# Attention inside a pre-norm block: weighing the shared key tile with split products

## What is computed

```
attn = jnp.where(valid, q @ k.T * scale, neg)      # valid: q_pos-128 < k_pos <= q_pos
attn = softmax(attn)
out  = attn @ v                                    # per head
x    = x + out @ wo
x    = x + ffn(layernorm(x))                       # ternary weights, exact gelu
```

## Time and profile before

| | us |
|---|---|
| median of 3 runs | 352.41 (350.9 to 352.82) |
| profiled execution, its own time | 355.15 |
| its span in the trace | 353.4 |
| TensorE busy | 340.2 (96% of the span) |
| VectorE busy | 270.7 (77%) |
| ScalarE busy | 206.6 (58%) |
| GpSimd busy | 224.0 (63%) |

### The profile page before, as it was taken

How to read it: one execution, slowest core, us unless ns; L and a number is a source line. 1 busy time by engine, 2 the same in 40 slices (tenths; PEclk the granted TensorE clock), 3 DMA queues, 4 the chain that set the end, 5 groups by cost and what they waited for, 6 DMA issues and landing times.

```text
span 353.4 us, 6926 instructions
## 1 busy us (share of the span) xinstructions
PE 340.2 (96%) x2410; PEld 315.9 (89%) x2410; DVE 270.7 (77%) x605; ACT 206.6 (58%) x628; POOL 224.0 (63%) x182
## 2 busy tenths in 40 slices
PE   7887989999999999999999999999999999989996
PEld 7876768999999999999999999999999999968986
DVE  4875867768876887889888987787788876878682
ACT  2424855687677556655665566656665566466280
POOL 2325878667767678898898897676767487230400
PEclk9989989999999999999999999999999999999999
DMA  7826465543333333333333333333322232000001
GB/s 220 213 58 173 127 166 152 130 105 78 91 86 81 81 86 87 92 89 92 89 91 89 91 90 91 92 90 76 91 54 56 57 89 61 0 3 0 32 30 59
DMA packets 29025, 31.25 MB, mean 88 GB/s; under 512 B 3392, under 2 KB 20288, under 8 KB 28992
## 3 DMA queue, kind: packets, MB, share of 16 engines
q1 hardware_dynamic: 28992, 30.82, 34.0%
HBM read 12.98 MB, written 1.05 MB: 40 GB/s over the span
## 4 chain that ended last, share of the span: by engine, by line
PE 85%; DVE 6%; POOL 3%; DMA 3%; issue 1%; ACT 1%; SPq 0%; POOLq 0%; DVEq 0%
PE PR L397 23%; PE OT L476 13%; PE SC L449 12%; PE VO L414 12%; PE VO L431 12%; PE PT L460 4%; PE PR L504 2%; PE VO L511 2%; PE SC L504 2%; DMA swapped<-by_sin 2%; POOL gT_lo L992 1%; PE SC L511 1%; POOL turn L987 1%; DMA xres<-in_x 1%; DVE stats L726 1%
## 5 line engine op out<-in xcount | busy, mean ns | idle before, releaser
L992 POOL TENSOR_TENSOR gT_lo<-turn,gT_hi 128x512 fp32r<-128x512 f32 x62 | 82.2, 1325 | 47.2 <-ACT gT_hi L622 47.0
L987 POOL TENSOR_TENSOR turn<-turn,swapped 128x512 f32<-128x512 f32 x62 | 80.2, 1293 | 25.7 <-DMA swapped<-by_sin 25.1
L627 ACT ACTIVATE probs<-SC,negmax 128x128 f32<-128x128 f32 x128 | 45.8, 363 | 80.6 <-DVE negmax L790 80.6
L801 DVE TENSOR_TENSOR probsT<-PT,mask_sb 128x512 f32<-128x512 f32 x64 | 44.1, 690 | 40.2 <-PE PT L460 40.1
L476 PE MATMUL OT<-probsT,v_sb 128*128 128x128 f32 x450 | 60.4, 276 | 1.6 <-DVE probsT L801 0.9
L476 PEld LDWEIGHTS OT<-probsT,v_sb 128*128 128x128 f32 x450 | 55.2, 191 | 2.9 <-DVE probsT L801 2.8
L634 ACT ACTIVATE probs<-probs,rinv 128x128 f32<-128x128 f32 x128 | 44.5, 394 | 19.1 <-DVE rinv L795 19.0
L397 PE MATMUL PR<-xT_hi,qk_lo 128*128 128x512 f32 x128 | 51.7, 404 | 2.0 <-DVE xT_lo L747 2.0
L397 PE MATMUL PR<-xT_lo,qk_hi 128*128 128x512 f32 x128 | 51.1, 399 | 0.0
L397 PE MATMUL PR<-xT_hi,qk_hi 128*128 128x512 f32 x128 | 50.9, 398 | 0.0
L449 PE MATMUL SC<-gT_hi,gT_lo 128*128 128x256 f32 (+1 forms) x128 | 41.5, 324 | 3.0 <-POOL gT_lo L992 3.0
(11 more groups left out here) (118 smaller groups left out, 841.7 us busy)
## 6 DMA issues: line engine op xcount, KB each, us to landing
swapped<-by_sin SPq DMA_DIRECT2D x128, 128.0 KB, 2.3
qk_raw<-in_wq SPq DMA_DIRECT2D x16, 128.0 KB, 2.6
qk_raw<-in_wk SPq DMA_DIRECT2D x16, 128.0 KB, 2.5
v_raw<-in_wv SPq DMA_DIRECT2D x8, 256.0 KB, 2.9
o_raw<-in_wo SPq DMA_DIRECT2D x8, 256.0 KB, 3.0
xres<-in_x SPq DMA_DIRECT2D x4, 256.0 KB, 3.3
w_raw<-in_w1t SPq DMA_DIRECT2D x4, 256.0 KB, 3.2
w_raw<-in_w2t SPq DMA_DIRECT2D x4, 256.0 KB, 3.1
```

The source lines that it names most:

```text
L627: nc.scalar.activation(probs[n % 2][:, i], SC[n % 2][:, i * 256 + P:(i + 1) * 256], ACT.Exp, bias=negmax[:, n % 2, i:i + 1], accum_out=row ...
L801: tt(probsT[:], PT[:, 0:256].rearrange("p (i q) -> p i q", i=2).unsqueeze(2).broadcast_to([P, 2, 2, P]), mask_sb[:].unsqueeze(1).broadcast ...
L987: tt(turn[m % 4][:], turn[m % 4][:], swapped[m % 2][:], ALU.add).then_inc(rot_done, 1)
L992: tt(rot_lo(head, c % 2)[:, half_of(c)], turn[m % 4][:], rot_hi(head, c % 2)[:, half_of(c)].bitcast(F32), ALU.subtract).then_inc(rotlo_don ...
```

## The change

In steps 8 to 59, `weigh_v` splits the work by key tile. The shared tile `2j` is multiplied with both query tiles at once, in three F32R products of 256 columns. The tiles `2j-1` and `2j+1` stay float32 products of 128 columns. So a step issues three split and two float32 products (one float32 product at `j = 0`) where it issued four (three) float32 products.

The halves that this needs are new. For the probabilities, ScalarE casts columns 128 to 383 of `probsT` (`pt_hi`, after `ot_hi` and ahead of the exponentials), and VectorE subtracts (`pt_lo`, after `merge` and ahead of `ot_lo`). For the even value tiles 4 to 29, ScalarE makes the high half from PSUM ahead of the copy in `copy_v`, and VectorE the low half (`v_low`) at the place of `add_out`. The PSUM bank of such a value tile is handed on when `v_low` is done, and `weigh_v` waits for both low halves.

```diff
+        both_hi = sb("both_hi", [P, 2 * P], F32R)
+        both_lo = sb("both_lo", [P, 2 * P], F32R)
+        v_even_hi = sb("v_even_hi", [P, NT // 2, 2 * HD], F32R)
+        v_even_lo = sb("v_even_lo", [P, NT // 2, 2 * HD], F32R)
...
+        def in_halves(n):
+            return 8 <= n < STEPS - 4
+        def even_split(v):
+            return 4 <= v < 4 * PAIRS - 2
...
             def bank_free(kind, i):
-                    pe.wait_ge(*((v_copied, user[1] + 1) if user[0] == "v" else (wo_added, o_at[user[1]] + 1)))
+                    pe.wait_ge(*((v_split, user[1] - 3) if user[0] == "v" and even_split(user[1])
+                              else (v_copied, user[1] + 1) if user[0] == "v" else (wo_added, o_at[user[1]] + 1)))
...
             def weigh_v(n):
+                if in_halves(n):
+                    pe.wait_ge(v_split, 4 * (head // 2) + j - 3)
+                    pe.wait_ge(both_lo_done, n - 7)
+                    mm(o[:, 0:256], v_even_hi[:, j, hs], both_hi[:], start=True, stop=False)
+                    mm(o[:, 0:256], v_even_lo[:, j, hs], both_hi[:], start=False, stop=False)
+                    mm(o[:, 0:256], v_even_hi[:, j, hs], both_lo[:], start=False, stop=False)
+                    if j > 0:
+                        mm(o[:, 0:P], v_sb[:, 2 * j - 1, hs], probsT[:, 0, 0], start=False, stop=False)
+                    last = mm(o[:, P:256], v_sb[:, 2 * j + 1, hs], probsT[:, 1, 1], start=False, stop=True)
+                else:
+                    pe.wait_ge(pt_masked, n + 1)
...
             def copy_v(v):
+                if even_split(v):
+                    copy(v_even_hi[:, c], VO[v % 2][:, 0:256]).then_inc(v_even_high, 1)
...
+            def pt_hi(n):
+                act.wait_ge(pt_masked, n + 1)
+                copy(both_hi[:], probsT[:].rearrange("p i b q -> p (i b q)")[:, P:3 * P]).then_inc(both_hi_done, 1)
...
                     ot_hi(n - 2)
+                if in_halves(n - 1):
+                    pt_hi(n - 1)
                 exps(n)
...
+            def v_low(v):
+                c = v % 4
+                dve.wait_ge(v_even_high, v - 3)
+                dve.wait_ge(v_copied, v + 1)
+                tt(v_even_lo[:, c], VO[v % 2][:, 0:256], v_even_hi[:, c].bitcast(F32), ALU.subtract).then_inc(v_split, 1)
+            def pt_lo(n):
+                dve.wait_ge(both_hi_done, n - 7)
+                tt(both_lo[:], probsT[:].rearrange("p i b q -> p (i b q)")[:, P:3 * P], both_hi[:].bitcast(F32),
+                   ALU.subtract).then_inc(both_lo_done, 1)
...
+                if in_halves(n - 1):
+                    pt_lo(n - 1)
                 if 1 < n < STEPS - 2:
                     ot_lo(n - 2)
...
                         if kind == "o" and n > 0:
                             add_out(w)
+                        if kind == "v" and even_split(w):
+                            v_low(w)
```

More of the change, by code:

```diff
@@ L164, in preln_block_kernel @@
         v_copied = sem("v_copied")
+        v_even_high = sem("v_even_high")
+        v_split = sem("v_split")
+        both_hi_done = sem("both_hi_done")
+        both_lo_done = sem("both_lo_done")
         wo_done = sem("wo_done")
@@ L465, in weigh_v @@
                 a = head % 2
-                pe.wait_ge(pt_masked, n + 1)
+                hs = slice(a * HD, (a + 1) * HD)
+                o = ot_bank(n)
                 pe.wait_ge(v_copied, 4 * (head // 2) + j + 1)
@@ L471, in weigh_v @@
                     pe.wait_ge(otlo_done, {4: 3, 5: 4, 6: 2}.get(n, n))
[L472 to L477, removed]
+                if in_halves(n):
[9 more added lines that the diff above has]
+                    pe.wait_ge(pt_masked, n + 1)
+                    for i in range(2):
+                        t = 2 * j + i
+                        b0 = 1 if t == 0 else 0
+                        for b in range(b0, 2):
+                            last = mm(ot_bank(n)[:, i * P:(i + 1) * P], v_sb[:, t - 1 + b, a * HD:(a + 1) * HD],
+                                      probsT[:, i, b], start=(b == b0), stop=(b == 1))
                 last.then_inc(pv_done, 1)
```

## The result

The changed kernel takes 365.36 us (median, 365.0 to 365.94), the kernel before in the same comparison 352.62. The ratio is 1.0376 with a 95% interval of 1.034 to 1.0411: slower by 12.7 us. Forecast were 366.4 us and slower.

The account below looks back on a forecast made before the run. TensorE, busy throughout the changed steps, was taken as the bound. Cheaper products -5.2, small terms +1 and VectorE blocked by GpSimd +18.2 sum to +14 us: a median of 366.4 us, 8-in-10 range 354 to 388.

Parts of the forecast that it names:

- TensorE's gain: In 52 changed steps, three split products replace two float32 ones, 0.10 us less each: -5.2 us if TensorE never waits.
- small terms of ScalarE and the ternary steps: Extra cast in value-tile steps, 1 us at most, and value low half in eight ternary steps, 2 at most: together +1.
- The taking of turns: VectorE with both operands in SBUF and GpSimd hold each other off, first to start wins; on the probabilities' low half, +18.2 us.
- Length of a blocked step, R + 3.36: Step whose probabilities' low half waits for GpSimd's rotation, begun R into the step: lasts R + 3.36 us, free ones 4.53.
- The alternation: After a free step the next low half is blocked, after a blocked one either: half of 52 steps, 0.70 us each.
- The sum: Whole kernel: -5.2 + 1 + 18.2 = +14 us, giving a median of 366.4 us, 4.0% slower.
- No lock: Rival: turns do not bite on the probabilities' low half, or few steps are blocked; 348.2 us, chance 0.14.
- Always blocked: Rival: the rotation precedes the low half every time, each step takes 5.41 us; +41.6 us, 394, chance 0.10.
- Mostly free: Rival: rotation's data land later, blocked share 0.10 to 0.25; -0.6 to +4.9 us, 352 to 357, chance 0.12.

Follow-up runs that it names:

- Run 1: Changed kernel with the low half of the probabilities taken from unmasked transposed probabilities in PSUM, so without the mask there; 346.94 us against 351.6, 0.9861.
- run 8: Changed kernel with two VectorE neighbours exchanged, the probabilities' low half behind the output's low half; 370.81 us against 352.5 for the kernel before, 1.0532.
- run 5: Changed kernel with the probabilities' halves and split products in even steps only, 26 in place of 52; 360.06 us against 351.38 for the kernel before, 1.0228.
- run 7: Changed kernel with the probabilities' low half made by GpSimd, between the rotation's low half and the rotation; 352.46 us against 351.38 for the kernel before, 1.0022.
- run 9: Changed kernel with the probabilities' low half put ahead of the row maximum, inside the merge; 358.48 us against 352.5 for the kernel before, 1.018.

## Why the prediction was right

- **TensorE's gain, -5.2 us.** In the changed kernel the weighing goes from 223.48 to 224.28, 0.80 against 0.90 before. Run 1 shows -3.9 over the 52 steps, which with the small terms of ScalarE and the ternary steps is -5.2 + 1.3; forecast was +1 with bounds 0 and 3. Right.
- **The taking of turns.** Run 1 against the changed kernel isolates it, the operand's place alone: 19.0 us, forecast 18.2. Ahead of the change it was shown only for another operation, of which the trace of before has eight: four of them are held, ending 0.54 to 0.55 after an instruction of GpSimd. The Trainium skill, page "SBUF — State Buffer", section "Who interferes with whom", extends it to tensor_tensor, and the trace agrees: 1.28 us at 226.33, 0.41 in run 1.
- **Length of a blocked step, R + 3.36.** At 224.28, R is 1.76: 5.12 expected, 5.12 measured. It holds to 0.01 us in 21 of the 24 blocked steps; in two the rotation's low half was what blocked, and the third is the last of the stretch. The 24 average 5.30, the free ones 4.45.
- **The alternation.** The share is 24 of 52, 0.46, forecast 0.5. Behind a free step 21 of 28 are blocked, forecast 0.8. Behind a blocked one only 3 of 23, where I had 0.3. That term was off because the mask comes at +0.48 instead of +0.54 when TensorE had to wait, and the low half with it at +2.00, while the rotation comes at +2.05 or +2.06: 0.06 behind it where I had 0.03. In the first step of a head (that from 229.40 is one) I had the rotation 0.02 ahead; it is 0.01 behind. A blocked step is dearer in turn: 19.0 / 24 is 0.79 each, against 0.70. In five of them a ternary instruction had pushed the mask back to +0.86 to +1.32. So 24 x 0.79 stands where 26 x 0.70 was forecast, and that the product is within 0.8 us is in part luck.
- **The sum.** +15.1 in the stretch against +14. The forecast of 366.4 is 1.0 above the median.
- **Small misses.** TensorE's idle time in the stretch is 251.65 - 240.26 = 11.4 us, where I had 15 to 20. In the kernel before, the rotation covers VectorE's instruction in 42 steps and not 43, if one counts the 52 steps from 64.09 to 300.63; the window in the earlier trace rows begins a step too early. Neither moves the sum.
- **The rivals.** "No lock" would be right but for the place of one operand: run 1 is this rival, at 346.9 where 348.2 was put on it. "Always blocked" is what run 8 comes near to by its share, 40 of 52, though not by its time: its blocked steps take 5.14 on average where the rival had 5.41. "Mostly free" did not occur.

Where my reasoning was weaker is in the expectations for runs 5, 7 and 9, as told there. The taking of turns held in each, but in run 5 the share and the price of a blocked step were off, and in runs 7 and 9 another engine's wait came in.

## What to carry to other kernels

Before giving VectorE an instruction, look where its tensors lie. With one operand in PSUM it cost nothing that could be measured here, with both in SBUF it ran against GpSimd and cost 19 us over 52 uses of 0.41 us. If it must be so, find out by the other engine's rows what runs at that moment: one place down VectorE's list moved the time from 1.038 to 1.053, one place up brought it to 1.018. A reserve per step is to be worked out for each kind of step, since copies that occur in half of them may eat it.

## What the runs showed of the hardware

- The delay is not proportional: a held instruction of VectorE with both operands in SBUF ends 0.28 to 0.29 us (256 columns) or 0.54 to 0.55 us (512 columns) after GpSimd's, whenever it was issued. All 24 long ones of the changed kernel and all 40 of run 8 do so.
- A waiting instruction of VectorE nearly always comes next, even when GpSimd has another one ready: in the changed kernel one from 144.34 waited for GpSimd's of 143.61, and GpSimd's next, of 144.85, then took 1.75 us. One case in these traces is different: in run 7 two instructions of GpSimd passed it, 3.85 us in place of 0.74. What decides it was not tried.
- GpSimd is held off as well, 1.56 instead of 1.29 us by one of 256 columns (231.44 in the changed kernel), 1.70 by one of 512.
